# Order of the dense up products, scores and heads in the draining steps of a fused attention, expert and feed-forward layer

## The chip, the cores and the metric

The kernel runs on one core of a Trainium2 chip. The metric is the device time of one execution in microseconds. Engines: TensorE (PE, its weight loads PEld), VectorE (DVE), ScalarE (ACT), GpSimd (POOL), and SyncE (SP), which issues most of the DMAs. Each engine works through its own list of instructions in the order in which it was written; semaphores are all that ties one list to another.

## What is computed

Input x has 16 batches of 256 tokens of width 128. It is normalised, and two branches of it are added to it:

```python
xn = _layernorm(x, axis=-1)
x = x + attention_layer(xn, ...) + experts(xn, ...)

# attention_layer, 16 heads of 8, 4 key/value heads, window of 32 tokens
h = _layernorm(x, g1, b1)
q, k = _rope(q), _rope(k)
attn = softmax(where(valid, q @ k / sqrt(HD), -1e9))
x = x + (attn @ v @ Wo + bo)
h2 = _layernorm(x, g2, b2)
return x + gelu(h2 @ Wf1 + bf1, approximate=False) @ Wf2 + bf2   # the dense part, DFF = 512

# experts: each token goes to its best 2 of 8
inter = silu(x @ w1.T) * (x @ w3.T) * g
y = inter @ w2.T
```

## The kernel before

After a first phase (normalising, queries, keys and values, routing) the kernel runs 19 steps, k = 0 to 18, each written out for every engine in a function `step` or `drain`. In steps 0 to 11 (`MSTEPS` = 12) every step takes six tiles of expert work along. Steps 12 to 18 are the draining steps (`drain`): no expert products are left, and the dense part (up products, gelu, down products) runs between what is left of the attention. It has 8 groups i of 512 tokens (two batches each).

Each step works on several batches at once. In step k: the scores of batch k, choosing, maximum, shift and exponentials of batch k, the transposed heads (queries, keys, values) of batch k+1, the bias and rotation of batch k+2, the products of weights and values of batch k-1 (`attend`) and their division by the sums (`norm`), the output product and residual of batch k-2 (`project`, `residual`), and the transposed second norm of batch k-3 (`h2_of`, `transpose_h2`, `take_h2T`). The batches end at 15, so steps 16 to 18 have ever less of it.

Below, a function with a batch and a half names one piece: scores(12,1) is the second half of the scores of batch 12. The pieces that count:

- TensorE, `scores` (lines 1261 and 1265) writes banks 0 and 1 and, for half 1, waits for `chosen` of half 0, that is for VectorE to have read those banks. `heads` (1245 to 1247) waits for the norm of batch k-1, since it writes the same bank. `up(i, chunks)` (1361) makes two chunks of 512 columns in banks 4 and 5; a chunk waits for the gelu two chunks before it. `down(i)` (1372), 32 matmuls, waits for all four gelus of the group. `project` is line 1312, `transpose_h2` 1274, `attend` 1297.
- ScalarE, `keep_own` (1050) copies the scores to `S`, after VectorE's transposes of the earlier weights (`pT_ready`). `take_keys` (1032) and `take_queries` (1039) copy the heads. `gelu` (1091) empties the up banks. `exps` (1056). `take_h2T` (1022).
- VectorE, `choose` (716) needs both keep_own and scores of that half; then maximum (723) and shift (728). `weights_T` (736) and `newer_part` (742) are the step's first work. `residual` (767) waits for `project`; `norm` (760, 762); `finish` (839) adds the down products of a group; `add_experts` (829) adds its expert rows.

Where the dense work stands is written out by hand in tables at the top: `UP_AT`, `DOWN_AT`, `FINISH_AT`, `EXPERTS_AT` and `RESID_AT` map (step, place) to a group; `tail(0)` to `tail(6)` are the seven places of a draining step, and `UP_AT` gives a pair of chunks. The same table places the up products on TensorE and the gelus on ScalarE. SP stores each `on` and loads it back as `outT`, loads the expert rows, and stores the output, each as its semaphores allow.

Of the kernel before, what the change touches and what calls it, by code (L numbers as in the profile page):

```python
# [44 lines left out]
MSTEPS = 12  # L45
# [12 lines left out]
NO_PAIR = 1e6  # L58
NEG = -1e30
UP_AT = {(MSTEPS, 0): (0, (0, 1)), (MSTEPS, 1): (0, (2, 3)), (MSTEPS, 2): (1, (0, 1)), (MSTEPS, 4): (1, (2, 3)),  # L60
         (MSTEPS + 1, 0): (2, (0, 1)), (MSTEPS + 1, 3): (2, (2, 3)),
         (MSTEPS + 2, 0): (3, (0, 1)), (MSTEPS + 2, 1): (3, (2, 3)), (MSTEPS + 2, 2): (4, (0, 1)), (MSTEPS + 2, 4): (4, (2, 3)),
         (MSTEPS + 3, 0): (5, (0, 1)), (MSTEPS + 3, 3): (5, (2, 3)),
         (MSTEPS + 4, 3): (6, (0, 1)), (MSTEPS + 4, 6): (6, (2, 3)),
         (MSTEPS + 6, 4): (7, (0, 1)), (MSTEPS + 6, 5): (7, (2, 3))}
DOWN_AT = {(MSTEPS, 3): 0, (MSTEPS, 5): 1, (MSTEPS + 1, 5): 2, (MSTEPS + 2, 3): 3, (MSTEPS + 2, 5): 4, (MSTEPS + 4, 0): 5,
# [8 lines left out]
def layer(nc, x, xt, wqkv, bqkv, wo, bo, g1, b1, g2, b2, wf1, bf1, wf2, bf2, gate, w13, w2,  # L75
          ident, center, cosf, sinf, older, newer, qmask, vmask, tri, rev, tilegrid, places, column, xn, ys, turned, out):
    F32, F16, BF16, I32 = mybir.dt.float32, mybir.dt.float16, mybir.dt.bfloat16, mybir.dt.int32
    ALU, ACT, AX = mybir.AluOpType, mybir.ActivationFunctionType, mybir.AxisListType
    ds = bass.ds
    ctx = ExitStack()  # L80
    with ctx:
        def sb(name, shape, dt=F32):
            return ctx.enter_context(nc.sbuf_tensor(name, shape, dt))[:]
# [15 lines left out]
        spare_act = sb("spare_act", [P, 1])  # L99
# [24 lines left out]
        eps_sb = sb("eps_sb", [P, NT])  # L124
# [162 lines left out]
        def exists(b):  # L287
            return not isinstance(b, int) or 0 <= b < B
# [661 lines left out]
        def _(act):  # L950
# [69 lines left out]
            def take_h2T(b):  # L1020
                act.wait_ge(h2T_psum, b + 1)
                nc.scalar.activation(h2T_sb[:, ds(b * T, T)], turn_bank[:, 0:T], ACT.Identity, bias=b2c, scale=g2c
                                     ).then_inc(h2T_ready, 1)

            def take_keys(b, p, half):
                if half == 0:
                    act.wait_ge(heads_psum, b + 1)
                    if some(b - 1):
                        act.wait_ge(scores_psum, 2 * (b - 1))
                for g in range(2 * half, 2 * half + 2):  # L1030
                    rows = slice(g * 32, (g + 1) * 32)
                    last = nc.scalar.activation(kT[rows, p, g, WIN:WIN + T], turn_bank[rows, T:2 * T], ACT.Copy)
                if half == 1:
                    last.then_inc(kT_ready, 1)

            def take_queries(b, p, half):

                for h in range(2 * half, 2 * half + 2):
                    last = nc.scalar.activation(qbd[:, p, :, h, :], turn_bank[:, 0:T].rearrange("p (n q) -> p n q", q=WIN),
                                                ACT.Copy, scale=qmask_sb[:, h:h + 1])  # L1040
                if half == 1:
                    last.then_inc(qbd_ready, 1)

            def keep_own(b, h):
                act.wait_ge(scores_psum, 2 * b + h + 1)
                if some(b):
                    act.wait_ge(pT_ready, 2 * b)
                half = S[:, h].rearrange("p (n g k) -> p n g k", n=HALF, g=G)
                for r in range(2):
                    last = nc.scalar.activation(half[:, :, 2 * r:2 * r + 2, :],  # L1050
                                                bank[r].rearrange("p (n g c) -> p n g c", n=HALF, g=2)[:, :, :, WIN:2 * WIN], ACT.Copy)
                last.then_inc(own_kept, 1)

            def exps(b):
                act.wait_ge(shifted, 2 * b + 2)
                nc.scalar.activation(S, S, ACT.Exp).then_inc(exp_ready, 1)
# [27 lines left out]
            def gelu(i, chunks):  # L1084
                if i == 3:
                    act.wait_ge(qkv_biased, B)
                for c in chunks:
                    act.wait_ge(up_psum, FC * i + c + 1)
                    if i >= 4:
                        act.wait_ge(down_psum, i - 3)  # L1090
                    nc.scalar.activation(gT[i % 4][:, c, :], bank[4 + c % 2], ACT.Gelu, bias=cols_sb[:, 4 + c:5 + c]  # L1091
                                         ).then_inc(gelu_ready, 1)

            def gates(m, i):
                if within(TILES * m + i):
                    silu(m, i, i % 2)
                if within(TILES * m + i + 1):
                    take_xsT(m, i + 1, (i + 1) % 2)

            def products(m, i):  # L1100
                if some(TILES * m + i + 1):
                    take_y(m, i)

            def next_silu():
                nc.scalar.activation(spare_act, eps_sb[:, 0:1], ACT.Silu)

            def step(k, p):
                gates(k, 0)
                products(k, -1)
                gates(k, 1)  # L1110
                keep_own(k, 0)
                products(k, 0)
                take_keys(k + 1, 1 - p, 0)
                gates(k, 2)
                take_keys(k + 1, 1 - p, 1)
                products(k, 1)
                take_queries(k + 1, 1 - p, 0)
                gates(k, 3)
                keep_own(k, 1)
                products(k, 2)  # L1120
                take_queries(k + 1, 1 - p, 1)
                gates(k, 4)
                products(k, 3)
                if exists(k - 3):
                    take_h2T(k - 3)
                gates(k, 5)
                exps(k)
                products(k, 4)
                if not (isinstance(k, int) and k == MSTEPS - 1):
                    next_silu()  # L1130

            def drain(k, p):

                def tail(i):
                    if (k, i) in UP_AT:
                        gelu(*UP_AT[k, i])

                if exists(k):
                    keep_own(k, 0)
                tail(0)  # L1140
                if exists(k + 1):
                    take_keys(k + 1, 1 - p, 0)
                    take_keys(k + 1, 1 - p, 1)
                tail(1)
                if exists(k + 1):
                    take_queries(k + 1, 1 - p, 0)
                    take_queries(k + 1, 1 - p, 1)
                if exists(k):
                    keep_own(k, 1)
                tail(2)  # L1150
                take_h2T(k - 3)
                tail(3)
                tail(4)
                if exists(k):
                    exps(k)
                tail(5)
                tail(6)

# [18 lines left out]
        def _(pe):  # L1177
# [175 lines left out]
            def up(i, chunks=range(FC)):  # L1353
                pe.wait_ge(h2T_ready, 2 * i + 2)
                for c in chunks:
                    if FC * i + c >= 2:
                        pe.wait_ge(gelu_ready, FC * i + c - 1)
                    elif c == 0:
                        pe.wait_ge(silu_ready, USED)
                        pe.wait_ge(inter_ready, USED)  # L1360
                    nc.tensor.matmul(bank[4 + c % 2], wf1_sb[:, c * P:(c + 1) * P], h2T_sb[:, i * 512:(i + 1) * 512],  # L1361
                                     start=True, stop=True).then_inc(up_psum, 1)
# [51 lines left out]
            def drain(k, p):  # L1414

                def tail(i):
                    if (k, i) in UP_AT:
                        up(*UP_AT[k, i])
                    if (k, i) in DOWN_AT:
                        down(DOWN_AT[k, i])  # L1420

                if exists(k):
                    scores(k, p, 0)
                if exists(k + 1):
                    heads(k + 1)
                tail(0)
                tail(1)
                if exists(k):
                    scores(k, p, 1)
                tail(2)  # L1430
                if exists(k + 1):
                    pe.wait_ge(kT_ready, k + 2)
                    pe.wait_ge(qbd_ready, k + 2)
                elif exists(k - 2):
                    pe.wait_ge(pv_normed, k - 1)
                transpose_h2(k - 3)
                tail(3)
                if exists(k - 1):
                    attend(k - 1, 1 - p, 0, k - 2)
                    attend(k - 1, 1 - p, 1, k - 2)  # L1440
                tail(4)
                if exists(k - 2):
                    project(k - 2, k + 2 if exists(k + 1) else B)
                if exists(k - 1):
                    attend(k - 1, 1 - p, 2, k - 2)
                    attend(k - 1, 1 - p, 3, k - 2)
                tail(5)
                tail(6)
# [95 lines left out]
```

## Time and profile before

| | |
|---|---|
| time, median of 3 runs | 435.57 us |
| lowest and highest | 434.14, 435.97 us |
| the profiled execution's own time | 436.67 us |
| its span in the trace | 434.8 us |
| granted TensorE clock, mean | 0.948 |
| steps 12 to 18 | from about 325 us to the end |

The profile is of one execution. A timeline merges instructions of one line that follow each other: "1.96 ... x4" is four instructions that took 1.96 us from the first start to the last end. A bracket at the end of a row is idle time of that engine before it, with what ended it; "issue" means that the trace shows no releaser. An fp32 product appears as more than one matmul. Draining steps are found by their first instructions: step 12 at 325.48 on TensorE, step 13 at 348.92, step 14 at 364.66, step 15 at 389.01.

### The profile page before, as it was taken

To read this page: it belongs to the slowest core of one execution; us is meant where nothing else is said; L and a number is where in the kernel's file an instruction comes from. 1 tells how busy PE (TensorE), PEld (TensorE's weight loads), DVE (VectorE), ACT (ScalarE), POOL (GpSimd) and SP (SyncE) were. 2 spreads that over 40 slices of the span, in tenths; PEclk is the share of its full clock that TensorE was granted. 3 is DMA by queue.
4 is the path that set the end of the run, shared out by engine and by line. 5 is a ranking of instruction groups with operands and counts; after the bars stand their busy time and mean duration, and the time that the engine had idled before them with its cause. 6 is when DMAs were issued, how large, how long until landed. Compare 5 with 4: busy or idle time off the path is not lost.

```text
span 434.8 us, 11754 instructions
## 1 busy us (share of the span) xinstructions
PE 385.7 (89%) x3647; PEld 346.1 (80%) x3648; DVE 356.8 (82%) x924; ACT 282.3 (65%) x711; POOL 197.9 (46%) x222
## 2 busy tenths in 40 slices
PE   4987629949999999999999999999997978997796
PEld 4977629949899999999999999899983846575563
DVE  0488644978999899999999999988988789969963
ACT  3795518757676877777777777767776572837222
POOL 2659132635646766676666665756621000000010
PEclk9995858979999999999999999999999999899889
DMA  8811683624656666565756565655503412303401
GB/s 249 233 50 55 209 286 110 201 62 142 196 152 183 194 179 178 178 185 171 207 174 176 177 175 181 177 164 174 179 20 90 131 25 86 86 15 84 121 26 48
DMA packets 59442, 62.25 MB, mean 143 GB/s; under 512 B 23182, under 2 KB 46610, under 8 KB 59280
## 3 DMA queue, kind: packets, MB, share of 16 engines
q1 hardware_dynamic: 53712, 52.69, 41.5%
q0 software_dynamic: 4544, 8.86, 6.7%
q8 instruction: 19, 0.31, 0.3%
q10 hardware_dynamic: 1152, 0.27, 0.3%
q14 instruction: 15, 0.12, 0.1%
HBM read 51.44 MB, written 10.81 MB: 143 GB/s over the span
## 4 chain that ended last, share of the span: by engine, by line
PE 67%; DVE 18%; issue 6%; DMA 4%; ACT 4%; POOL 1%; DVEq 0%; ACTq 0%; POOLq 0%
PE bank L1331 15%; PE bank L1348 13%; PE bank L1338 10%; PE bank L1261 6%; PE bank L1361 5%; PE bank L1297 3%; PE bank L1372 3%; DVE rsum L760 2%; DMA xsb<-scratch_xn,token 2%; PE bank L1184 2%; PE bank L1322 2%; PE bank L1206 2%; DVE x_sb L829 2%; PE bank L1192 2%; DMA scratch_xn<-xn_sb 1%
## 5 line engine op out<-in xcount | busy, mean ns | idle before, releaser
L468 POOL DMA_INDIRECT scratch_ys<-ysb,pair x71 | 76.1, 1072 | 80.3 <-ACT ysb L1082 63.9
L461 POOL DMA_INDIRECT xsb<-scratch_xn,token x71 | 77.3, 1089 | 37.5 <-issue 16.8
L1331 PE MATMUL bank<-xsT,w_sb 128*128 128x128 f32 x568 | 80.2, 286 | 6.4 <-ACT xsT L1076 6.4
L1331 PEld LDWEIGHTS bank<-xsT,w_sb 128*128 128x128 f32 x568 | 70.6, 196 | 10.4 <-ACT xsT L1076 6.8
L1348 PE MATMUL bank<-w_sb,inter 128*128 x568 | 76.1, 278 | 1.2 <-issue 0.6
L1348 PEld LDWEIGHTS bank<-w_sb,inter 128*128 128x128 f32 x568 | 69.5, 193 | 2.1 <-issue 1.8
L1338 PE MATMUL bank<-xsT,w_sb 128*128 128x128 f32 x426 | 60.6, 280 | 1.4 <-DVE inter L797 1.4
L1338 PEld LDWEIGHTS bank<-xsT,w_sb 128*128 128x128 f32 x426 | 54.6, 196 | 1.8 <-issue 1.8
L1068 ACT ACTIVATE act<-bank 64x128 f32<-64x128 f32 x71 | 19.0, 268 | 39.8 <-PE bank L1331 37.7
L450 POOL TENSOR_TENSOR ve<-mv,eps_sb 128x2 f32<-128x2 f32 x16 | 4.4, 274 | 86.2 <-DVE mv L777 86.2
L801 DVE TENSOR_TENSOR inter<-bank,act 128x384 f32<-128x384 f32 x71 | 39.6, 557 | 2.4 <-ACT xsT L1076 0.2
L797 DVE TENSOR_TENSOR inter<-bank,act 64x128 f32<-64x128 f32 x71 | 20.9, 295 | 22.9 <-ACT act L1069 13.6
L1261 PE MATMUL bank<-kT,qbd 64*128 64x128 f32 x512 | 37.6, 287 | 1.4 <-DVE S L716 1.4
L1361 PE MATMUL bank<-h2T_sb,wf_sb 128*128 128x512 f32 x64 | 35.5, 684 | 3.5 <-ACT gT_sb L1091 2.2
L1261 PEld LDWEIGHTS bank<-kT,qbd 64*128 64x128 f32 x512 | 31.5, 190 | 8.2 <-issue 2.8
L1069 ACT ACTIVATE act<-bank 128x384 f32<-128x384 f32 x71 | 34.8, 491 | 0.9
L1050 ACT ACTIVATE S<-bank 128x256 f32<-128x256 f32 x64 | 21.1, 387 | 20.4 <-DVE pT L736 17.1
L1091 ACT ACTIVATE gT_sb<-bank,cols_sb 128x512 f32<-128x512 f32 x32 | 21.2, 693 | 18.8 <-PE bank L1361 18.7
L1372 PEld LDWEIGHTS bank<-wf_sb,gT_sb 128*128 128x128 f32 x256 | 29.2, 192 | 2.7 <-ACT gT_sb L1091 1.9
L1372 PE MATMUL bank<-wf_sb,gT_sb 128*128 128x128 f32 x256 | 30.5, 278 | 0.9 <-ACT gT_sb L1091 0.8
L1082 ACT ACTIVATE ysb<-bank 128x128 f32<-128x128 f32 x71 | 19.5, 274 | 15.4 <-PE bank L1348 13.4
L1076 ACT ACTIVATE xsT<-bank 128x128 f32<-128x128 f32 x71 | 19.6, 276 | 14.5 <-PE bank L1322 14.2
(178 smaller groups left out, 798.7 us busy)
## 6 DMA issues: line engine op xcount, KB each, us to landing
w_sb<-in_w SPq DMA_DIRECT2D x71, 448.0 KB
w_sb<-scratch_ys SPq DMA_DIRECT2D x16, 256.0 KB, 3.4
w_sb<-in_xt SPq DMA_DIRECT2D x8, 256.0 KB, 6.1
x_sb<-in_x SPq DMA_DIRECT2D x8, 256.0 KB, 6.7
scratch_xn<-xn_sb SPq DMA_DIRECT2D x8, 256.0 KB, 2.3
w_sb<-in_w SPq DMA_DIRECT2D x1, 2048.0 KB, 8.2
out_dram<-x_sb SPq DMA_DIRECT2D x8, 256.0 KB, 3.3
scratch_turned<-on SPq DMA_DIRECT2D x15, 128.0 KB
```

The lines of the kernel that those rows point to most:

```text
L461: nc.gpsimd.indirect_dma_start(xsb[:, j % 3, :], None, xn, bass.IndirectOffsetOnAxis(ap=token[:, j:j + 1], axis=0)).then_inc(slots_in[j % ...
L468: nc.gpsimd.indirect_dma_start(ys, bass.IndirectOffsetOnAxis(ap=pair[:, j:j + 1], axis=0), ysb[:, j % 3, :], None, bounds_check=2 * NTOK - ...
L801: nc.vector.tensor_tensor(inter[:, p, 0:FULL], h3_bank[i % 3][:, 0:FULL], act1[:, p, 0:FULL], ALU.mult).then_inc(inter_ready, 1)
L1050: last = nc.scalar.activation(half[:, :, 2 * r:2 * r + 2, :], bank[r].rearrange("p (n g c) -> p n g c", n=HALF, g=2)[:, :, :, WIN:2 * WIN] ...
L1069: nc.scalar.activation(act1[:, p, 0:FULL], h1_bank[i % 3][:, 0:FULL], ACT.Silu).then_inc(silu_ready, 1)
L1091: nc.scalar.activation(gT[i % 4][:, c, :], bank[4 + c % 2], ACT.Gelu, bias=cols_sb[:, 4 + c:5 + c]).then_inc(gelu_ready, 1)
L1261: last = nc.tensor.matmul(bank[r][:, i * GW:(i + 1) * GW], qbd[rows, p, n].rearrange("p h q -> p (h q)"), kT[rows, p, 2 * r:2 * r + 2, n * ...
L1331: last = nc.tensor.matmul(h1_bank[i % 3][:, c * P:(c + 1) * P], w13_sb[:, i % 3, c * P:(c + 1) * P], xsT[:, p, :], start=True, stop=True)
L1338: last = nc.tensor.matmul(h3_bank[i % 3][:, (c - EC) * P:(c - EC + 1) * P], w13_sb[:, i % 3, c * P:(c + 1) * P], xsT[:, p, :], start=True, ...
L1348: last = nc.tensor.matmul(y_bank[:, 0:D], inter[:, p, c * P:(c + 1) * P], w2_sb[:, ds(at + c * P, P)], start=(c == 0), stop=(c == EC - 1))
L1361: nc.tensor.matmul(bank[4 + c % 2], wf1_sb[:, c * P:(c + 1) * P], h2T_sb[:, i * 512:(i + 1) * 512], start=True, stop=True).then_inc(up_psu ...
L1372: last = nc.tensor.matmul(bank[6 + i % 2][:, t * D:(t + 1) * D], gT[i % 4][:, c, t * P:(t + 1) * P], wf2_sb[:, c, :], start=(c == 0), stop ...
```

## The change

In `drain` on ScalarE and on TensorE, `tail(0)` goes to the front: the first up pair of a step (and the down of group 5 in step 16), with its gelus, comes ahead of `keep_own(k, 0)` and of `scores(k, p, 0)` and `heads(k + 1)`. A dummy gelu, `next_gelu`, follows the exponentials at the end of step 11 and of steps 12 to 15. In steps 13 and 15 the second up pair moves from place 3 to place 2, that is ahead of `transpose_h2` and `take_h2T`. VectorE, GpSimd and SP are not edited.

```diff
--- before.py
+++ after.py
@@ -58,9 +58,9 @@
 NO_PAIR = 1e6
 NEG = -1e30
 UP_AT = {(MSTEPS, 0): (0, (0, 1)), (MSTEPS, 1): (0, (2, 3)), (MSTEPS, 2): (1, (0, 1)), (MSTEPS, 4): (1, (2, 3)),
-         (MSTEPS + 1, 0): (2, (0, 1)), (MSTEPS + 1, 3): (2, (2, 3)),
+         (MSTEPS + 1, 0): (2, (0, 1)), (MSTEPS + 1, 2): (2, (2, 3)),
          (MSTEPS + 2, 0): (3, (0, 1)), (MSTEPS + 2, 1): (3, (2, 3)), (MSTEPS + 2, 2): (4, (0, 1)), (MSTEPS + 2, 4): (4, (2, 3)),
-         (MSTEPS + 3, 0): (5, (0, 1)), (MSTEPS + 3, 3): (5, (2, 3)),
+         (MSTEPS + 3, 0): (5, (0, 1)), (MSTEPS + 3, 2): (5, (2, 3)),
          (MSTEPS + 4, 3): (6, (0, 1)), (MSTEPS + 4, 6): (6, (2, 3)),
          (MSTEPS + 6, 4): (7, (0, 1)), (MSTEPS + 6, 5): (7, (2, 3))}
 DOWN_AT = {(MSTEPS, 3): 0, (MSTEPS, 5): 1, (MSTEPS + 1, 5): 2, (MSTEPS + 2, 3): 3, (MSTEPS + 2, 5): 4, (MSTEPS + 4, 0): 5,
@@ -1104,6 +1104,9 @@
             def next_silu():
                 nc.scalar.activation(spare_act, eps_sb[:, 0:1], ACT.Silu)
 
+            def next_gelu():
+                nc.scalar.activation(spare_act, eps_sb[:, 0:1], ACT.Gelu)
+
             def step(k, p):
                 gates(k, 0)
                 products(k, -1)
@@ -1126,7 +1129,9 @@
                 gates(k, 5)
                 exps(k)
                 products(k, 4)
-                if not (isinstance(k, int) and k == MSTEPS - 1):
+                if isinstance(k, int) and k == MSTEPS - 1:
+                    next_gelu()
+                else:
                     next_silu()
 
             def drain(k, p):
@@ -1135,9 +1140,9 @@
                     if (k, i) in UP_AT:
                         gelu(*UP_AT[k, i])
 
+                tail(0)
                 if exists(k):
                     keep_own(k, 0)
-                tail(0)
                 if exists(k + 1):
                     take_keys(k + 1, 1 - p, 0)
                     take_keys(k + 1, 1 - p, 1)
@@ -1153,6 +1158,7 @@
                 tail(4)
                 if exists(k):
                     exps(k)
+                    next_gelu()
                 tail(5)
                 tail(6)
 
@@ -1419,11 +1425,11 @@
                     if (k, i) in DOWN_AT:
                         down(DOWN_AT[k, i])
 
+                tail(0)
                 if exists(k):
                     scores(k, p, 0)
                 if exists(k + 1):
                     heads(k + 1)
-                tail(0)
                 tail(1)
                 if exists(k):
                     scores(k, p, 1)
```

## Rows read from the trace of the kernel before

**Rows 1.** The page: busy time of each engine, and the chain that ended last.
```profile
PE 385.7 (89%) x3647; PEld 346.1 (80%) x3648; DVE 356.8 (82%) x924; ACT 282.3 (65%) x711; POOL 197.9 (46%) x222
...
PE 67%; DVE 18%; issue 6%; DMA 4%; ACT 4%; POOL 1%; DVEq 0%; ACTq 0%; POOLq 0%
```

**Rows 2.** Timeline of VectorE, steps 12 and 13: start, us, instruction, idle before and releaser.
```profile
331.75 0.43 DVE L716 COPY_PREDICATED S<-older_sb,bank 128x256 f32<-128x256 int32 x1
...
337.70 0.44 DVE L716 COPY_PREDICATED S<-older_sb,bank 128x256 f32<-128x256 int32 x1 [2.40 <-issue]
...
344.47 0.42 DVE L767 TENSOR_TENSOR xn_sb<-bank,xn_sb 128x256 f32<-128x256 f32 x1 [1.64 <-PE bank L1312]
...
350.98 0.44 DVE L716 COPY_PREDICATED S<-older_sb,bank 128x256 f32<-128x256 int32 x1
...
357.10 0.44 DVE L716 COPY_PREDICATED S<-older_sb,bank 128x256 f32<-128x256 int32 x1 [1.66 <-issue]
```

**Rows 3.** Timeline of VectorE, steps 14 and 15.
```profile
371.84 0.43 DVE L716 COPY_PREDICATED S<-older_sb,bank 128x256 f32<-128x256 int32 x1
...
381.40 0.69 DVE L839 TENSOR_TENSOR x_sb<-bank,x_sb 128x512 f32<-128x512 f32 x1 [1.40 <-PE bank L1372]
384.56 0.42 DVE L767 TENSOR_TENSOR xn_sb<-bank,xn_sb 128x256 f32<-128x256 f32 x1 [2.46 <-PE bank L1312]
...
392.73 0.43 DVE L716 COPY_PREDICATED S<-older_sb,bank 128x256 f32<-128x256 int32 x1
```

**Rows 4.** Timeline of ScalarE, step 12.
```profile
329.72 0.66 ACT L1050 ACTIVATE S<-bank 128x256 f32<-128x256 f32 x2 [4.21 <-DVE pT L736]
330.40 1.28 ACT L1091 ACT_TABLE_LOAD   x1
331.69 1.26 ACT L1091 ACTIVATE gT_sb<-bank,cols_sb 128x512 f32<-128x512 f32 x2
332.85 1.52 ACT L1032 ACTIVATE kT<-bank 32x256 f32<-32x256 f32 x4
...
336.97 0.69 ACT L1050 ACTIVATE S<-bank 128x256 f32<-128x256 f32 x2
```

**Rows 5.** Timeline of TensorE, steps 12 to 15: scores, and one up pair.
```profile
325.48 1.16 PE L1261 MATMUL bank<-kT,qbd 64*128 64x128 f32 x16
...
334.41 1.16 PE L1261 MATMUL bank<-kT,qbd 64*128 64x128 f32 x16
...
348.92 1.16 PE L1261 MATMUL bank<-kT,qbd 64*128 64x128 f32 x16
...
350.77 1.88 PE L1361 MATMUL bank<-h2T_sb,wf_sb 128*128 128x512 f32 x4
...
374.50 1.16 PE L1261 MATMUL bank<-kT,qbd 64*128 64x128 f32 x16
...
389.01 1.16 PE L1261 MATMUL bank<-kT,qbd 64*128 64x128 f32 x16
```

**Rows 6.** Timeline of ScalarE, step 13: the two keep_own.
```profile
350.28 0.66 ACT L1050 ACTIVATE S<-bank 128x256 f32<-128x256 f32 x2 [3.20 <-PE bank L1265]
...
356.39 0.67 ACT L1050 ACTIVATE S<-bank 128x256 f32<-128x256 f32 x2
```

**Rows 7.** The tile spare_act (dummy silu), then ScalarE's timeline in step 16.
```profile
L1105 ACT ACTIVATE spare_act<-eps_sb x11: 202/203/203, 87.8 to 307.3; 128x1 f32<-128x1 f32 x11
...
406.31 1.28 ACT L1091 ACT_TABLE_LOAD   x1
408.17 0.69 ACT L1091 ACTIVATE gT_sb<-bank,cols_sb 128x512 f32<-128x512 f32 x1 [0.58 <-PE bank L1361]
```

**Rows 8.** Stretches: us, busy of each engine, granted clock (PEclk), DMA.
```profile
353.70:356.60 2.90, 0.04 (x2) 0.02 (x1) 1.71 (x5) 2.84 (x9) 0.00 (x0) 1.00 0.01 3
...
368.60:374.50 5.90, 5.17 (x12) 1.63 (x10) 5.80 (x13) 4.60 (x10) 0.00 (x0) 0.71 0.21 44
...
406.00:411.00 5.00, 4.65 (x15) 2.68 (x16) 4.90 (x12) 2.95 (x4) 0.00 (x0) 0.66 0.17 26
```

## The prediction

> **What bounds the kernel now.** Read the page first: TensorE is busy for 89% of the span and VectorE for 82%, and the chain that ended last is 67% PE and 18% DVE [rows 1]. These are averages; the change touches only the draining steps 12 to 18, from 325 us on. So the next view is VectorE's timeline in that stretch. Nearly all of a draining step is VectorE work in one fixed order (softmax of one batch, rotation of another, norms, residuals, expert sums), and it runs without a gap except in a few places. The reader is to look for the brackets. In step 12 it stands 2.40 us before `choose(12,1)` and 1.64 us before `residual(10)`; in step 13 it stands 1.66 us before `choose(13,1)` [rows 2]. In step 14 it stands 1.40 us before `finish(3)` and 2.46 us before `residual(12)` [rows 3]. In steps 15 and 16 there is no gap of note. What could be gained is therefore at most these 9.6 us.
>
> Next, who ends each gap. `choose(b,1)` needs `keep_own(b,1)`, which is ScalarE's. ScalarE's timeline of step 12 shows why it is late: keep_own(12,0) at 329.72, then a table load of 1.28 us, then two gelus of 1.26 us, then the keys at 332.85, and only at 336.97 the second keep_own [rows 4]. Step 13 has the same sequence: keep_own(13,0) at 350.28 and keep_own(13,1) at 356.39 [rows 6]. `residual` needs `project`, which is TensorE's, and TensorE's timeline shows it to be 10.06 us of unbroken matmuls after the start of scores(b,1): 344.47 - 334.41 in step 12 and 384.56 - 374.50 in step 14 [rows 2, 3, 5]. Those scores stood behind the second up pair, which waited for the bank that the late first gelu empties. So the table load and first gelus delay both chains.
>
> **Part 1: the table load goes behind the exponentials.** `next_gelu` adds one load and one tiny activation per step, and takes away the load before the first gelu. The same dummy exists for silu and takes 202 ns [rows 7]. Five loads go and five come; +0.2 us each on ScalarE. At the end of step 11 ScalarE has nothing to do until 329.72 (4.21 us idle) [rows 4], so the load is free there; in steps 12 to 15 it stands behind `exps`, where the trace shows ScalarE waiting for the next keep_own, 3.20 us in step 13 [rows 6]. A load doesn't wait for its activation's operand: at 406.31 it ran at once and its gelu started at 408.17 when TensorE was ready [rows 7]. If cover were gone (keep_own ready as soon as exps end), it would cost 1.49 us in each step; the gaps say it isn't. I take 0.
>
> The Trainium skill ("ScalarE: Activation LUTs", What ACT_TABLE_LOAD costs) prices a switch at about 2.66 us, a drain included; here the load took 1.28 us and the gelu began 1.29 us after it [rows 4]. By the page's price each load hidden would free 1.38 us more of ScalarE, but VectorE's gap of 2.40 us caps what step 12 can use, and the sum stays.
>
> **Part 2: the first up pair and its gelus ahead of scores and heads.** Step 12. On TensorE the pair (1.88 us by its row) starts at 325.48 instead of the scores; scores(12,0) then end by 328.7, heads(13), which waited for a norm until 328.5 anyway, are late by about 0.1 us. Both gelus are done by 328.4, before keep_own(12,0), which waits for VectorE's transposes at 329.7. So the keys start at 330.40 instead of 332.85 and keep_own(12,1) at 330.40 + (336.97 - 332.85) = 334.52, done at 335.2 [rows 4]. VectorE reached its wait at 337.70 - 2.40 = 335.30: the gap is gone, -2.40 at that point. What is late next is TensorE. Its second up pair runs at 329.4 without waiting, and scores(12,1) now wait for choose(12,0), done at 332.18 [rows 2]. They start at 332.25; plus 10.06 gives residual(10) at 342.31 against 344.47: **-2.16**.
>
> Step 13. TensorE stays busy: before, scores(13,0) began 4.45 us after residual(10). Now the up pair begins there, at 346.76, and the scores at 348.64. This is the price of the new order: 1.88 us on a path that VectorE is waiting for. From scores to keep_own(13,0) it took 350.28 - 348.92 = 1.36, so 350.00, and choose(13,0) starts 0.70 later, at 350.70 against 350.98: only -0.28, though VectorE would be ready at 348.82 [rows 2, 5, 6]. 1.88 of the 2.16 is given back. But now keep_own(13,1) comes 356.39 - 350.28 - 2.54 = 3.57 after keep_own(13,0), at 353.57, ready at 354.27; VectorE reaches it at 357.10 - 1.66 - 0.28 = 355.16 [rows 2, 4, 6] (2.54 is the load and the gelus). The gap of 1.66 is gone: **-1.94**.
>
> Step 14. Everything starts 1.94 earlier. There is no gap before choose(14,1) to gain. choose(14,0) ends at 372.27 - 1.94 = 370.33 [rows 3]. Scores(14,1) stood at 374.50, again behind the late gelu and the second up pair; now both are long done (heads(15) wait for norm(12), which moves by 1.94, and the pair follows them near 366.6 and ends by 368.5), so they start at 370.40. finish(3) waits no more. Plus 10.06: residual(12) at 380.46 against 384.56: **-4.10**.
>
> Step 15. As in step 13 the up pair goes in front: it begins at 389.01 - 4.10 = 384.91, scores at 386.79, keep_own(15,0) at 388.15, choose(15,0) at 388.88, where VectorE would be ready at 388.63: 0.25 given back, **-3.85** [rows 3, 5]. From here VectorE has no gap to lose or win before step 17, and TensorE's transposes wait for VectorE; all moves by 3.85. In step 16 the load before up 6 is gone too, but its gelu waited 0.58 us for TensorE after the load [rows 7]: nothing.
>
> **Part 3: the second pair of groups 2 and 5 one place ahead.** In step 13 TensorE stood for 2.9 us up to 356.6 [rows 8], waiting for the queries before it could transpose h2(10); the pair (1.88) now fills that. Its two gelus (1.26) go in front of h2T(10) on ScalarE, and attend(12) is queued on TensorE behind that. I take 0: ScalarE is 2.5 us earlier there than before, and residual(11), which waits for attend and project, had no gap before it, with the shift, the rotation and an expert sum still in front of it on VectorE. Were that cover gone it would cost the two gelus, 1.26 us. In step 15 likewise. No queue of SP or POOL is passed; the store of `on` and the loads of `outT` follow VectorE's norms and move with them.
>
> **The sum.** Profiled execution: span 434.8 - 3.85 = 431.0, its own time 436.67 - 3.85 = 432.8. That execution lay 1.10 over the median of the runs shown, so against the median 435.57 - 3.85 = **431.7 us**.
>
> **The rivals.** (a) The clock. TensorE is the bound in 332 to 350 and 370 to 381. The granted clock fell to its lower level (1.2 GHz instead of 2.4) for a part of three stretches: means of 0.71 over 5.9 us from 368.6, of 0.66 over 5.0 us from 406.0, and a third from 413.6; each costs up to 5.9 x 0.29 = 1.7 us of full-speed work. The first came after TensorE stood 2.0 us, yet 2.9 us of standing at 353.7 was followed by none [rows 8]. After the change TensorE stands some 1.8 us just before 370.4, and a fall there hits the bound: 431.7 + 1.7 = 433.4. Before, the fall at 368.6 cost little, as the gelu waited for its table anyway. The skill's "TensorE: Matmul & The Clock Gate" (What's actually happening) says the slow clock is the default and activity releases it; by it the new order would slow wherever it makes TensorE stand, which is this rival. (b) The falls at 406 and 413.6 were on the chain; if the new timing misses both, 3.4 us more go: 428.3. (c) Half the credit only: PE wins nothing in step 14, because up(3) or its gelu is held elsewhere (it waits for the last bias addition; that VectorE does this soon after choose(13,1), at 355.2, speaks against it). Then the gain stays at 1.94, less 0.25 in step 15: 433.9. (d) It doesn't do what it says: the gelu table is loaded again before the first gelu. The load would still stand before keep_own, in its shadow: about the forecast less 0.5; not held apart. (e) Slower: scores behind the up pair. In steps 13 and 15 that order puts 1.88 us of dense work in front of the item VectorE waits for, and it is paid for only by the TensorE time won in 12 and 14. If the clock falls for spells like those seen in both stretches, twice in each, TensorE loses 4 x 1.7 = 6.8 and the gain of 3.85 turns into +2.9: 438.5. It decides once more than 3.85 us are lost there; before, none fell in 330 to 350, which speaks against it.
>
> **How the numbers follow.** Forecast 0.63 (430.5 to 433); clock on the bound (a) 0.15; fewer slow spells (b) 0.07; half credit (c) 0.10; slower (e) 0.05. A measurement can tell about 0.5%, 2.2 us, from no change. The forecast and (b) are faster, (a) at 2.2 us of gain is faster about half the time, (c) is no change: faster 0.78, same 0.17, slower 0.05. For the range, (b) is left out below except its half-way, (e) above, and the rest is in: 429.6 to 434.2; the unknown costs (0.2 us dummies, 0.1 us waits) are within it.
>
> **What would show it.** In the trace after: the gelu load directly behind each exp; keep_own(12,1) near 334.5 and no gap before choose(12,1) and choose(13,1); scores(12,1) right behind choose(12,0); residual(10) near 342.3 and residual(12) near 380.5, still with gaps of 1.7 to 1.9 us before them; TensorE's up pair directly before scores(13,0), and a new VectorE gap of about 1.9 us before choose(13,0). Wrong would be: gelus still behind a load, scores(14,1) not at the end of choose(14,0), or a low granted clock after 370.

## The result

| | before | after |
|---|---|---|
| time, median | 435.57 us (434.14 to 435.97, 5 runs) | 431.92 us (429.85 to 432.40, 5 runs) |
| ratio | | 0.9907, 95% interval 0.9882 to 0.9932 |
| profiled execution, own time and span | 436.67, 434.8 us | 431.92, 430.1 us |

The change saves 0.93% (0.7 to 1.2), 4 us. The profiled executions differ by 4.7 us. To compare the draining steps alone, positions below are counted from one instruction that stands before anything changed: the start of norm(10) on VectorE, its reciprocal of 1.73 us at the end of step 11. It is at 326.24 before and at 324.77 after:

```profile
326.24 1.73 DVE L760 RECIPROCAL rsum<-bank 128x256 f32<-128x256 f32 x1
```

```profile
324.77 1.72 DVE L760 RECIPROCAL rsum<-bank 128x256 f32<-128x256 f32 x1
```

So 1.47 us of the 4.7 lie ahead of the change, in code that it doesn't touch. I take them for this pair of executions and not for the change: 1.46 are there already at norm(9), a step earlier (306.67 and 305.21), the medians of the runs differ by 3.65 only, and in four further traces below with the same code up to there norm(10) starts anywhere from 323.82 to 325.61. From norm(10) to the end of the span it is 108.56 us before and 105.33 after: 3.2 us. The page after: TensorE 90%, VectorE 83%, and the chain has hardly moved [rows 1]:

```profile
PE 385.3 (90%) x3647; PEld 347.4 (81%) x3648; DVE 356.6 (83%) x924; ACT 283.6 (66%) x716; POOL 198.1 (46%) x222
...
PE 69%; DVE 16%; issue 6%; DMA 4%; ACT 4%; SPq 0%; DVEq 0%; ACTq 0%; POOLq 0%
```

VectorE's timeline after; the answers to [rows 2] and [rows 3]:

```profile
333.77 0.44 DVE L716 COPY_PREDICATED S<-older_sb,bank 128x256 f32<-128x256 int32 x1
...
340.83 0.42 DVE L767 TENSOR_TENSOR xn_sb<-bank,xn_sb 128x256 f32<-128x256 f32 x1 [1.94 <-PE bank L1318]
...
349.07 0.43 DVE L716 COPY_PREDICATED S<-older_sb,bank 128x256 f32<-128x256 int32 x1 [1.74 <-issue]
...
353.45 0.43 DVE L716 COPY_PREDICATED S<-older_sb,bank 128x256 f32<-128x256 int32 x1
...
376.16 0.68 DVE L839 TENSOR_TENSOR x_sb<-bank,x_sb 128x512 f32<-128x512 f32 x1
378.74 0.42 DVE L767 TENSOR_TENSOR xn_sb<-bank,xn_sb 128x256 f32<-128x256 f32 x1 [1.90 <-PE bank L1318]
...
386.98 0.43 DVE L716 COPY_PREDICATED S<-older_sb,bank 128x256 f32<-128x256 int32 x1
```

The reader is to see which brackets are gone: before choose(12,1) (333.77), before choose(13,1) (353.45) and before finish(3) (376.16). Two stay, 1.94 us before residual(10) and 1.90 before residual(12), and a new one of 1.74 us stands before choose(13,0) at 349.07. ScalarE after, for [rows 4] and [rows 6]:

```profile
324.06 1.28 ACT L1108 ACT_TABLE_LOAD   x1
325.36 0.20 ACT L1108 ACTIVATE spare_act<-eps_sb 128x1 f32<-128x1 f32 x1
325.47 1.26 ACT L1091 ACTIVATE gT_sb<-bank,cols_sb 128x512 f32<-128x512 f32 x2
328.26 0.66 ACT L1050 ACTIVATE S<-bank 128x256 f32<-128x256 f32 x2 [1.54 <-DVE pT L736]
328.81 1.52 ACT L1032 ACTIVATE kT<-bank 32x256 f32<-32x256 f32 x4
...
332.94 0.69 ACT L1050 ACTIVATE S<-bank 128x256 f32<-128x256 f32 x2
...
348.37 0.66 ACT L1050 ACTIVATE S<-bank 128x256 f32<-128x256 f32 x2 [0.57 <-PE bank L1271]
...
352.06 0.68 ACT L1050 ACTIVATE S<-bank 128x256 f32<-128x256 f32 x2
```

The table load runs at 324.06, behind the last expert copy, and the first gelus are over before keep_own(12,0) at 328.26; nothing stands between it and the keys. TensorE after, for [rows 5]:

```profile
330.77 1.16 PE L1267 MATMUL bank<-kT,qbd 64*128 64x128 f32 x16 [1.11 <-DVE S L716]
...
345.19 1.88 PE L1367 MATMUL bank<-h2T_sb,wf_sb 128*128 128x512 f32 x4
347.00 1.16 PE L1267 MATMUL bank<-kT,qbd 64*128 64x128 f32 x16
...
368.68 1.16 PE L1267 MATMUL bank<-kT,qbd 64*128 64x128 f32 x16 [1.75 <-DVE S L716]
...
404.96 0.71 PE L1318 MATMUL bank<-wo_sb,outT 128*128 128x128 f32 x4 [0.89 <-DMA outT<-scratch_turned]
```

Scores(12,1) at 330.77 and scores(14,1) at 368.68 now wait for VectorE's choose (1.11 and 1.75 us of standing) and for nothing else. At 345.19 the up pair stands in front of scores(13,0).

In positions from norm(10), in us ("forecast" is the prediction's own time for the item less 326.24, and for residual(14) and what follows the position before less 3.85):

| | before | forecast | after |
|---|---|---|---|
| choose(12,1) | 11.46 | 9.06 | 9.00 |
| residual(10) | 18.23 | 16.07 | 16.06 |
| choose(13,0) | 24.74 | 24.46 | 24.30 |
| choose(13,1) | 30.86 | 28.92 | 28.68 |
| residual(12) | 58.32 | 54.22 | 53.97 |
| choose(15,0) | 66.49 | 62.64 | 62.21 |
| residual(14) | 87.40 | 83.55 | 83.13 |
| residual(15) | 91.69 | 87.84 | 88.43 |
| end of span | 108.56 | 104.71 | 105.33 |

### The profile page after: what moved, and what is told of

The parts are those of the page before. It is cut to its first block, busy times and chain, and to the rows that moved or that the text cites. A ratio compares the mean times of both kernels' runs of the same rounds, so it can differ in the third digit from the quotient of the medians.

```text
span 430.1 us, 11759 instructions
## 1 busy us (share of the span) xinstructions
PE 385.3 (90%) x3647; PEld 347.4 (81%) x3648; DVE 356.6 (83%) x924; ACT 283.6 (66%) x716; POOL 198.1 (46%) x222
## 4 chain that ended last, share of the span: by engine, by line
PE 69%; DVE 16%; issue 6%; DMA 4%; ACT 4%; SPq 0%; DVEq 0%; ACTq 0%; POOLq 0%
PE bank L1337 15%; PE bank L1354 14%; PE bank L1344 10%; PE bank L1267 6%; PE bank L1367 4%; PE bank L1303 3%; PE bank L1190 3%; PE bank L1198 3%; PE bank L1378 3%; DVE rsum L760 2%; PE bank L1328 2%; PE bank L1212 2%; DVE x_sb L829 2%; DMA scratch_xn<-xn_sb 1%; PE bank L1318 1%
## 5 line engine op out<-in xcount | busy, mean ns | idle before, releaser
L1367 PE MATMUL bank<-h2T_sb,wf_sb 128*128 128x512 f32 x64 | 33.0, 640 | 1.3 <-ACT h2T_sb L1022 1.3
L1032 ACT ACTIVATE kT<-bank 32x256 f32<-32x256 f32 x64 | 24.0, 375 | 4.4 <-PE bank L1253 3.7
```

## The experiments

The experiments ran on three chips, each ratio against the kernel before on the same chip. On one (the old order in steps 13 and 15, the doubled pairs and the pairs behind project) the kernel before took 436.13 us. On the two others (one for the first trace of every other experiment, one for the second) it took some 468 us: every kernel ran some 30 us longer, nearly all of it ahead of step 12, and runs of one kernel spread over about 3%; there the ratios say little and the traces decide. From norm(10) to residual(14) the two traces of one kernel agree to 0.02 us wherever its matmuls ran at the full clock.

**The dummies alone.** The kernel before with `next_gelu` added; both `tail(0)` calls and the table are as before:

```diff
+                if isinstance(k, int) and k == MSTEPS - 1:
+                    next_gelu()
...
                     exps(k)
+                    next_gelu()
```

> Only the dummy gelus are added; the order is that of the kernel before. Theory (the late first gelu is the cause, by its table load as much as by its place): in step 12 the first gelus end at 331.9 instead of 332.95, scores(12,1) start 1.4 us earlier because the bank comes free at 331.1, residual(10) 1.4 us earlier; choose(13,0) 1.4, choose(13,1) 1.5, residual(12) and all after it 2.9 us earlier than before, relative to the start of step 12. Time about 432.7. Rival (the place in the order is what counts, a load hidden alone brings nothing): within 0.5 us of before, 435.1 to 435.6.

> The kernel with the dummies alone, timed again, since the runs of the first chip spread over 3%. From its trace there (residual(14) 2.75 us earlier than before): theory 0.9937, that is 2.75 of 436; rival (the loads alone bring nothing) 1.000.

Ratios 0.9975 (0.9933 to 1.0017) and 0.9926 (0.9885 to 0.9967). VectorE's timeline of the second, with norm(10) at 360.56:

```profile
360.56 1.73 DVE L760 RECIPROCAL rsum<-bank 128x256 f32<-128x256 f32 x1
...
370.90 0.44 DVE L716 COPY_PREDICATED S<-older_sb,bank 128x256 f32<-128x256 int32 x1 [1.26 <-issue]
...
390.08 0.43 DVE L716 COPY_PREDICATED S<-older_sb,bank 128x256 f32<-128x256 int32 x1 [1.52 <-issue]
...
416.12 0.42 DVE L767 TENSOR_TENSOR xn_sb<-bank,xn_sb 128x256 f32<-128x256 f32 x1 [2.46 <-PE bank L1318]
```

About half of the gap before choose(12,1) is gone (1.26 us left of 2.40), little of that before choose(13,1) (1.52 of 1.66), and the 2.46 before residual(12) still stands, though that comes at 55.56, 58.32 - 55.56 = 2.76 us earlier than before. residual(14) is 2.73 earlier, 2.75 in the first trace. The theory had 2.9, with 1.4 at residual(10), where 1.21 were measured. The loads alone carry some 2.7 of the 4.27 us that the change brings up to residual(14). On these chips, where the kernel before takes 468 us, 2.7 us are a ratio of 0.994, inside both intervals; the rival's 1.000 lies outside the second.

One other cause could hide in this number: the kernel before had a low clock from 368.6 in step 14 [rows 8], and these two traces had none there. Its TensorE timeline says that it cost nothing:

```profile
372.62 1.96 PE L1361 MATMUL bank<-h2T_sb,wf_sb 128*128 128x512 f32 x4 [0.73 <-ACT gT_sb L1091]
```

The slowed pair was over and TensorE stood 0.73 us for the first gelu, which came right behind its table load (370.49 to 371.77).

**The order alone.** The changed kernel without `next_gelu`:

```diff
-                if isinstance(k, int) and k == MSTEPS - 1:
-                    next_gelu()
...
-                    next_gelu()
```

> The changed kernel without its dummy gelus. Theory (an ACT_TABLE_LOAD doesn't wait for its activation's operand, and with the first gelu next in ScalarE's list the load stands behind the exponentials by itself): the same table loads at the same places, time as the changed kernel within 0.5 us, 431.9; only in step 16 the load stands behind the transposed norm again, 1.28 us, of which 0.58 or more is hidden. Rival (the dummies bring the tables early and the order needs them): the load of 1.28 us stands before each first gelu once the up pair is done, up to 1.3 us back in each of steps 12 and 14, 433 to 434.5.

> The kernel with the order alone, timed again. Theory (the dummies do nothing once the gelus stand in front): 0.990, as the changed kernel's 0.9907, 4.27 us. Rival (the dummies are needed): 0.993 or more.

Ratios 0.9919 (0.9870 to 0.9967) and 0.9906 (0.9864 to 0.9948). In the first trace every position up to residual(14) is that of the changed kernel to 0.02 us (83.13). ScalarE's timeline of it, end of step 12:

```profile
376.05 1.06 ACT L1056 ACTIVATE S<-S 128x1024 f32<-128x1024 f32 x1
377.13 1.28 ACT L1091 ACT_TABLE_LOAD   x1
379.92 0.69 ACT L1091 ACTIVATE gT_sb<-bank,cols_sb 128x512 f32<-128x512 f32 x1 [1.50 <-PE bank L1364]
```

The load stands right behind the exponentials (377.13) without a dummy, ahead of step 13, while its gelu waits 1.50 us for TensorE; ahead of steps 12, 15 and of the up pair in step 16 it does the same. Ahead of step 14 it does not, and there the theory (the same loads at the same places) missed. From the same timeline:

```profile
395.16 1.28 ACT L1091 ACT_TABLE_LOAD   x1 [4.74 <-PE bank L1364]
...
399.83 0.66 ACT L1050 ACTIVATE S<-bank 128x256 f32<-128x256 f32 x2 [2.11 <-DVE pT L736]
```

The load itself stood 4.74 us until TensorE had made the first chunk of group 3, the same in the second trace (4.75). It cost nothing only because ScalarE still had 2.11 us to spare before keep_own(14,0). Group 3 is the one whose first gelu has a second wait written ahead of that for its up product (`qkv_biased`); whether this holds the load was not tested. So in time the dummies of the change do nothing and the order does it all, but not because every load runs ahead by itself.

The second trace of the same kernel shows something else. Position of residual(12): 55.66 instead of 53.97, 1.69 us later. TensorE's timeline, VectorE's, and two stretches (us, busy of each engine, granted clock, DMA):

```profile
397.22 1.88 PE L1364 MATMUL bank<-h2T_sb,wf_sb 128*128 128x512 f32 x4
400.85 1.16 PE L1264 MATMUL bank<-kT,qbd 64*128 64x128 f32 x16 [1.75 <-DVE S L716]
401.94 3.44 PE L1364 MATMUL bank<-h2T_sb,wf_sb 128*128 128x512 f32 x4
```

```profile
409.44 0.69 DVE L839 TENSOR_TENSOR x_sb<-bank,x_sb 128x512 f32<-128x512 f32 x1 [1.04 <-PE bank L1375]
412.59 0.42 DVE L767 TENSOR_TENSOR xn_sb<-bank,xn_sb 128x256 f32<-128x256 f32 x1 [2.46 <-PE bank L1315]
```

```profile
396.00:401.00 5.00, 2.72 (x12) 1.44 (x14) 4.92 (x10) 2.83 (x8) 0.00 (x0) 1.00 0.36 96
401.00:405.50 4.50, 4.50 (x22) 2.34 (x23) 4.36 (x14) 3.48 (x10) 0.00 (x0) 0.65 0.07 10
```

The up pair of step 14 took 3.44 us instead of 1.98, with a granted clock of 0.65 in 401 to 405.5, and VectorE's gap before residual(12) grew from 1.90 to 2.46, with 1.04 more before finish(3). This is the rival of the clock, at its place and near its price (1.7 was forecast). The ratio 0.9906 does not tell the theory's 0.990 from the rival's 0.993.

**The second pairs back at place 3.**

```diff
-         (MSTEPS + 1, 0): (2, (0, 1)), (MSTEPS + 1, 2): (2, (2, 3)),
+         (MSTEPS + 1, 0): (2, (0, 1)), (MSTEPS + 1, 3): (2, (2, 3)),
...
-         (MSTEPS + 3, 0): (5, (0, 1)), (MSTEPS + 3, 2): (5, (2, 3)),
+         (MSTEPS + 3, 0): (5, (0, 1)), (MSTEPS + 3, 3): (5, (2, 3)),
```

> The changed kernel with the second up pairs of steps 13 and 15 back at place 3, behind the transposed norms. Theory (this part is worth nothing on the path): attend(12) about 1 us later or the same, no VectorE gap before residual(11) or residual(13), time within 0.4 us of the changed kernel. Rival (TensorE is the bound in steps 13 and 15 too): 1.3 to 2 us slower, 433.2 to 434.

Ratio 0.9971 (0.9929 to 1.0013), from runs between 460.9 and 470.1 us. The trace is sharper: residual(12) 53.97, residual(13) 70.72, residual(14) 83.13, each as in the changed kernel. That part is worth nothing.

**The old order in steps 13 and 15 only.** On both engines:

```diff
-                tail(0)
+                early = k in (MSTEPS, MSTEPS + 2)
+                if early:
+                    tail(0)
```

and `if not early: tail(0)` behind keep_own on ScalarE and behind heads on TensorE.

> The changed kernel, but in steps 13 and 15 the first up pair and its gelus stand behind scores, heads and keep_own as before. Positions are counted from the start of norm(10) on VectorE (in the changed kernel: choose(13,0) 24.30, choose(13,1) 28.68, residual(12) 53.97, residual(14) 83.13). Theory (in step 13 the front place only moves the wait from choose(13,1) to choose(13,0)): choose(13,0) without a gap at 22.6, then a gap of about 1.7 us before choose(13,1), at 28.8; residual(14) within 0.3 us of 83.13. Rival (the front place in step 13 is part of the gain): residual(14) 1 us or more later, 84 or more.

432.55 us beside 436.13, ratio 0.9938 (0.9916 to 0.9961).

```profile
323.82 1.73 DVE L760 RECIPROCAL rsum<-bank 128x256 f32<-128x256 f32 x1
...
346.40 0.44 DVE L716 COPY_PREDICATED S<-older_sb,bank 128x256 f32<-128x256 int32 x1
...
352.40 0.44 DVE L716 COPY_PREDICATED S<-older_sb,bank 128x256 f32<-128x256 int32 x1 [1.54 <-issue]
```

choose(13,0) is at 22.58 without a gap, then 1.54 us of waiting before choose(13,1), at 28.58. residual(14) is at 82.97, even 0.16 earlier. In these two steps the new place brings nothing; it moves the wait. The gain of the change is that of steps 12 and 14.

**Step 13's first pair behind.** On top of the changed kernel:

```diff
-         (MSTEPS + 1, 0): (2, (0, 1)), (MSTEPS + 1, 2): (2, (2, 3)),
+         (MSTEPS + 1, 2): (2, (0, 1, 2, 3)),
```

> The changed kernel with step 13's first up pair moved behind scores(13,1) and keep_own(13,1), together with the second pair. Theory (in step 13 the up pair ahead of the scores costs 1.8 us of the gap of 1.74 us that VectorE now has before choose(13,0)): that gap is gone, choose(13,1) 1.7 us earlier, residual(12) and the rest 1.7 us earlier, time about 430.2. Rival (TensorE is the bound throughout, so that the pair only costs elsewhere): the same as the changed kernel within 0.5 us, with a gap of about 1.7 us before residual(11) or a larger one before residual(12).

> The kernel with step 13's first pair behind, timed again. Theory: 6.0 us less than before, 0.9862. Rival (that gain is lost behind residual(14)): 0.990.

Ratios 0.9932 (0.9886 to 0.9978) and 0.9919 (0.9885 to 0.9954). VectorE's timeline of the first, norm(10) at 356.55:

```profile
356.55 1.73 DVE L760 RECIPROCAL rsum<-bank 128x256 f32<-128x256 f32 x1
...
379.12 0.43 DVE L716 COPY_PREDICATED S<-older_sb,bank 128x256 f32<-128x256 int32 x1
...
383.51 0.44 DVE L716 COPY_PREDICATED S<-older_sb,bank 128x256 f32<-128x256 int32 x1
```

No bracket before choose(13,0) and choose(13,1); residual(12) at 52.24, residual(14) at 81.40: 1.73 us earlier than in the changed kernel, 6.00 earlier than before, the same in the second execution (81.41). On these chips' 468 us that is a ratio of 0.9872, just below both intervals (lower ends 0.9886 and 0.9885), so by the times alone the rival (0.990) fits better. In part the traces say why: at the end of the span the two executions are 5.21 and 6.44 us earlier than before, the first having lost 1.3 us between residual(14) and residual(15) to a low clock (see the rest of the drain, below). With such a spread between runs the times don't settle the rest. The last experiment contains the same edit on the faster chip.

**The same pair doubled.** Each matmul of step 13's first pair is issued twice, in the changed kernel and in the version with the pair behind:

```diff
+                    for twice in range(2 if i == 2 and c < 2 else 1):
+                        last = nc.tensor.matmul(bank[4 + c % 2], ...)
+                    last.then_inc(up_psum, 1)
```

> The changed kernel with each matmul of step 13's first up pair issued twice (the same product into the same bank), 1.9 us more on TensorE. Theory (TensorE is the bound from scores(12,1) to choose(13,0)): choose(13,0) at 24.30 + 1.8 = 26.1 from the start of norm(10), its gap 3.6 us, residual(14) 1.8 later, 84.9. Rival (VectorE's gap there is ScalarE's doing, or slack): less than 0.5 us later.

> The same doubled pair in the version where it stands behind scores(13,1). Theory (there TensorE has slack up to project(11)): no gap on VectorE, residual(14) at 81.40 as in that version, within 0.2 us. Rival (TensorE is short of time wherever the pair stands): 1 to 1.9 us later, a gap before residual(11).

Each ran once. VectorE's timeline with the pair doubled in front, norm(10) at 324.62:

```profile
350.63 0.43 DVE L716 COPY_PREDICATED S<-older_sb,bank 128x256 f32<-128x256 int32 x1 [3.45 <-issue]
```

In front of the scores, 1.9 us more on TensorE give a gap of 3.45 us, choose(13,0) at 26.01 and residual(14) at 84.84: 1.71 us later. Behind the scores, choose(13,1) stays at 26.96, but residual(14) is at 82.02, 0.62 later than without doubling. That is more than the theory had (0.2) and less than its rival (1 to 1.9, with a gap before residual(11), which did not come). TensorE's timelines behind, with the pair doubled and single:

```profile
366.59 1.88 PE L1368 MATMUL bank<-h2T_sb,wf_sb 128*128 128x512 f32 x4
368.40 1.16 PE L1267 MATMUL bank<-kT,qbd 64*128 64x128 f32 x16
```

```profile
396.29 1.88 PE L1367 MATMUL bank<-h2T_sb,wf_sb 128*128 128x512 f32 x4
398.74 1.16 PE L1267 MATMUL bank<-kT,qbd 64*128 64x128 f32 x16 [0.56 <-DVE S L716]
```

Single, scores(14,1) stood 0.56 us waiting for VectorE; doubled, it comes to them late and without a wait. Of the 1.8 us added behind, 0.6 reach residual(14), so the slack there is about 1.2 us, not the whole of step 13.

**Pairs behind project.** On top of the version with step 13's pair behind:

```diff
-UP_AT = {(MSTEPS, 0): (0, (0, 1)), (MSTEPS, 1): (0, (2, 3)), (MSTEPS, 2): (1, (0, 1)), (MSTEPS, 4): (1, (2, 3)),
+UP_AT = {(MSTEPS, 0): (0, (0, 1)), (MSTEPS, 1): (0, (2, 3)), (MSTEPS, 2): (1, (0, 1)), (MSTEPS, 5): (1, (2, 3)),
...
-         (MSTEPS + 2, 0): (3, (0, 1)), (MSTEPS + 2, 1): (3, (2, 3)), (MSTEPS + 2, 2): (4, (0, 1)), (MSTEPS + 2, 4): (4, (2, 3)),
+         (MSTEPS + 2, 0): (3, (0, 1)), (MSTEPS + 2, 1): (3, (2, 3)), (MSTEPS + 2, 2): (4, (0, 1)), (MSTEPS + 2, 5): (4, (2, 3)),
...
-DOWN_AT = {(MSTEPS, 3): 0, (MSTEPS, 5): 1, (MSTEPS + 1, 5): 2, (MSTEPS + 2, 3): 3, (MSTEPS + 2, 5): 4, (MSTEPS + 4, 0): 5,
+DOWN_AT = {(MSTEPS, 3): 0, (MSTEPS + 1, 1): 1, (MSTEPS + 1, 5): 2, (MSTEPS + 2, 3): 3, (MSTEPS + 3, 1): 4, (MSTEPS + 4, 0): 5,
```

> On top of the version with step 13's pair behind: the second up pairs of groups 1 and 4 behind project, and down(1) and down(4) behind the scores of the next step. Theory (the two gaps of 1.9 us before residual(10) and residual(12) are TensorE's 1.9 us up pair in front of project): both gaps close, residual(10) at 14.2 from the start of norm(10), residual(14) at 83.13 - 1.73 - 1.88 - 1.90 = 77.6; against the changed kernel 5.5 us less, against the kernel before 9.5 us less. Rival (TensorE has as much work as VectorE from step 12 to 15, and the work pushed back comes up later as a gap): a new gap before choose(13,1) or choose(15,0), half of the gain or less.

```profile
324.29 1.72 DVE L760 RECIPROCAL rsum<-bank 128x256 f32<-128x256 f32 x1
...
338.63 0.42 DVE L767 TENSOR_TENSOR xn_sb<-bank,xn_sb 128x256 f32<-128x256 f32 x1 [0.21 <-PE bank L1318]
...
345.06 0.44 DVE L716 COPY_PREDICATED S<-older_sb,bank 128x256 f32<-128x256 int32 x1
...
373.02 0.42 DVE L767 TENSOR_TENSOR xn_sb<-bank,xn_sb 128x256 f32<-128x256 f32 x1 [0.18 <-PE bank L1318]
```

Gaps of 0.21 and 0.18 us are left of 1.94 and 1.90, and no new one stands before choose(13,1) or choose(15,0), so the rival is out; residual(14) is at 77.84 for the theory's 77.6, that is 9.56 us earlier than before, of the 9.6 us of waits that the prediction called the most to be had. The time is **426.03 us** beside 436.13 on the same chip, ratio 0.9769 (0.9750 to 0.9788): 10.1 us less than before, the best version of this study. The traces have 8.55 of these behind norm(10) (108.56 before, 100.01 here); the rest lies ahead of it, as in the result.

## Why the prediction was right

**The size.** 431.7 forecast, 431.92 measured. The gain up to residual(14) was 4.27 us for 3.85 forecast; 1.0 of it is lost again by residual(15), and the gain at the end is 3.2 (below). So the forecast of 3.85 lies 0.4 us below the one and 0.6 above the other. The mechanism of steps 12 to 15 was right; that the median came within 0.2 us of the forecast is in part luck, since behind norm(10) a gain that was forecast too small and a loss that wasn't forecast at all nearly cancel.

**Part 1, the table load.** That ScalarE's load and gelus hold up both chains was right; the experiments split it: 2.75 us for the load out of the way, the rest up to 4.27 for the place. What the prediction missed is that the two aren't additive. It had the row that shows it, a load that runs ahead of its gelu's wait [rows 7], and still counted `next_gelu` as the means. Once the gelu is the next item of ScalarE's list behind exps, its load runs there by itself (377.13), except ahead of step 14, where it stood 4.74 us and was covered all the same.

**Part 2, step 12.** Gap 2.40 gone (forecast 2.40), residual(10) 2.17 earlier (2.16); its new gap is 1.94. **Step 13:** the price of the pair in front was forecast as 1.88 given back of 2.16, leaving 0.28; 0.44 were left. Two terms were over-sized: the pair holds TensorE for 1.81 us (345.19 to 347.00), not the 1.88 of its row, which counts the last matmul to its end (the trace before had the same: the pair starts at 350.77, the scores behind it at 352.58); and from residual(10) to the pair it was 4.36, not 4.45, as down(1) handed over to the pair after 3.67 us (341.52 to 345.19) where it had handed over to the scores after 3.77 before (345.15 to 348.92). choose(13,1) came 2.18 earlier for 1.94 forecast: these 0.16, and 0.08 in the VectorE work between, which took 4.38 us (349.07 to 353.45) for 4.46. The old order in step 13 confirms the give-back as such. **Step 14:** residual(12) 4.35 earlier for 4.10; the step itself brought 2.17 for 2.16. **Step 15:** 0.25 given back was forecast (386.79 + 1.36 + 0.70 makes 388.85 and not 388.88, so 0.22), 0.07 measured. The same two terms were too long by 0.16 there: keep_own(15,0) ended at 386.94, and choose(15,0) began at 386.98, about when VectorE was ready. **Part 3:** zero, as forecast, and shown.

**The rest of the drain.** "All moves by 3.85" is the sentence that failed. Up to residual(14) the whole drain moved as one, by the 4.27 above, but from there to residual(15) it is 5.30 us after and was 4.29 before, so 1.01 are lost: the prediction took this stretch as fixed. The path there goes over TensorE in step 16: the second half of attend, the second up pair of group 6, a transpose and project(15). TensorE also stood 0.89 us at 404.96 for the loads of `outT`, but that is not the loss: project(14) still came 4.91 us earlier than before, more than the 4.27 of residual(14). In the second trace of the version with step 13's pair behind the same stand is there, and residual(15) follows residual(14) (437.09) after 4.02 us, within 0.01 of the shortest in any trace:

```profile
434.19 0.71 PE L1318 MATMUL bank<-wo_sb,outT 128*128 128x128 f32 x4 [0.92 <-DMA outT<-scratch_turned]
...
441.11 0.42 DVE L767 TENSOR_TENSOR xn_sb<-bank,xn_sb 128x256 f32<-128x256 f32 x1 [0.99 <-PE bank L1318]
```

What differs is how much of this path ran at the low clock. Stretches of the changed kernel:

```profile
370.00:404.00 34.00, 29.40 (x274) 22.07 (x273) 31.09 (x84) 18.64 (x30) 1.79 (x4) 1.00 0.31 85
405.00:413.00 8.00, 8.00 (x30) 5.80 (x30) 5.52 (x21) 1.17 (x2) 0.89 (x2) 0.57 0.23 68
```

It was full from 370 to 404 and 0.57 in 405 to 413, over nearly the whole path; before, two spells lay at 406 and 413.6 [rows 8], with full clock between them. With the order alone, first trace, the one spell of step 16 came earlier, in the first up pair: residual(15) at 87.15 and the end at 103.77, where the changed kernel has 88.43 and 105.33. So the place of the spell decides 1.3 us at residual(15) and 1.6 at the end. It varies between executions of one kernel: the two traces of the order alone have 4.02 and 5.14 us from residual(14) to residual(15), those with the pair behind 5.29 and 4.02. Whether the change makes a long spell there likelier isn't shown. The rival of fewer spells priced the two spells before at 3.4 us; from residual(14) to the end it took 21.16 us before, and the shortest of all traces is 20.64, so a step 16 whose spell lay off this path was worth 0.5. No trace has a step 16 without any spell, so the 3.4 stays unconfirmed.

**The rivals.** The clock on the bound did not fall in this profile but did in the second trace of the order alone. Half credit in step 14: no, up(3) ran at 360.4 without a wait. Slower: one more pair in front of scores(13,0), 1.8 us of work, lost 1.71 us, so what stands there is paid nearly one to one, as the rival had it, but nothing of that size came.

**What stays open.** The 1.47 us ahead of norm(10), why two of the chips need 30 us more ahead of step 12, why the load ahead of step 14 waited, and what makes a spell of low clock come in one execution and not in another.

## What to carry to other kernels

Look at what stands between two gates that the busiest engine waits for, on each feeding engine, and move whole items past the gate; but an item put in front of work that the busiest engine needs next is paid nearly in full, so put it behind that work instead (here 1.73 us in step 13, and 3.6 us more for the two pairs behind project). A table load often starts as soon as the activation before it ends, though its own activation still waits (377.13, the gelu at 379.92); then the next function's activation need only be the next in the list. Where another activation stood between, a dummy brought 2.75 us. But look at each load in the trace: one here stood 4.74 us with its activation, and only the slack behind it made that free.

## What was not expected of the hardware

Positions on VectorE over 80 us of draining repeat to 0.02 us between executions and chips: the changed kernel at 430 us and its versions without the dummies or with the second pairs back at 462 and 463 us have residual(14) at 83.13 all three. Only a spell of low granted clock moved them between traces of one kernel. One spell in a stretch where TensorE is the bound cost 1.69 us (a mean of 0.65 over 4.5 us, so partly at 1.2 instead of 2.4 GHz); four other traces, the changed kernel's among them, with the same 1.75 us of standing before the same scores, had none. The Trainium skill ("TensorE: Matmul & The Clock Gate", Seeing it yourself) warns that the trace's clock events can be unreliable; here they agree with the durations, as the pair took 3.44 us in the spell and 1.98 outside it.
